# Four GNN layers on one Trainium2 core: graph attention applied ahead of its weight, score terms as row sums, norm shifts on GpSimd, and a new instruction order

## The chip, the core and the metric

The kernel runs on one core of one Trainium2 chip. The metric is device time in microseconds (us) of one execution; of several runs the median is taken. In the profile, PE is TensorE's matmuls, PEld its weight loads, DVE is VectorE, ACT is ScalarE, POOL is GpSimd and SP is SyncE, which here only issues DMAs.

## The reference, cut to what matters

The input x holds 128 graphs of 128 nodes with 256 features, and one 128x128 adjacency matrix `adj` serves all of them. Four layers follow each other; each normalizes its input, applies a ReLU, and adds its result to the input. The third, graph attention, is the one whose arithmetic the change reorders.

```
def layer_L2(h, W, a, beta, mask):
    hw = h @ W
    s1, s2 = hw @ a[:F], hw @ a[F:]
    e = leaky_relu(s1[:, :, None] + s2[:, None, :], 0.2) * mask
    att = softmax(e, axis=2)
    return elu(att @ hw + beta * hw)

h = relu(layernorm(x)); x = x + L0(h, ...)   # 8-head masked attention, projection, layernorm
h = relu(layernorm(x)); x = x + L1(h, ...)   # (adj.T * q k^T), rows divided by their norm, times v
h = relu(layernorm(x)); x = x + L2(h, ...)   # graph attention, above
h = relu(layernorm(x)); x = x + L3(h, ...)   # (adj @ h) @ weight + bias
```

## The kernel before, in words

Two graphs form a pair, and 64 pairs go through the four layers as a software pipeline. One pair's work is cut into steps, and in one turn of the main loop each engine does one step of each of about ten different pairs: in turn t, the name `p3` is pair t-3, and `on[3]` says whether it exists. The order of all instructions on each engine is written out by hand in the function `step` of that engine. Semaphores link the engines. An engine executes strictly in that order, so a wait holds up all that is written behind it. DVE's `step` of turn t+1 runs beside PE's of turn t for most of the work: the pair that DVE calls p1 is then PE's p0.

PSUM has 8 banks, four of them in the tile `mid`, whose four banks take the attention scores of the four row groups. All other products share these banks, and `bank_free` waits for the last reader of a bank.

The steps that matter here, for one pair:

- `moments` (DVE: two `bn_stats`, two `bn_aggr`) and `inverse_root` (POOL: `var_eps`, then `rstd` by a power) make a norm's mean and scale. A small DVE instruction makes `shift` = -mean * rstd (lines 792, 849, 814, 858 for norms 0, 1, 2, 3). ACT then writes the normalized rows z (two instructions per pair), PE transposes them (`transposes`, 4), ACT writes the high part `h_t_hi` with the ReLU, and DVE or POOL the low part `h_t_lo`.
- `product` is a product in two parts (high and low) with 3 matmuls for each of two 128-row pieces. `rows` and `columns` take 12 such matmuls of 256 columns per pair.
- Scores (line 365, 32 small matmuls) go to `mid`; `least_masked` on DVE (line 751, four groups r of four instructions) adds the mask and takes the minimum; ACT's `exps` (line 562) make `probs` and their sums; POOL divides by the sums; PE transposes (line 356); ACT copies to `probs_t`; PE multiplies with the values (line 377, `heads_times_values`).
- Graph attention: z2 is transposed (4 PE transposes), `h_t[2]` is made in two parts, `rows` gives hw with two further columns for the terms s1 and s2 (12 matmuls of 258 columns), ACT copies hw (line 681, two instructions), PE spreads the s2 term (line 431), ACT applies the leaky ReLU, POOL the mask, DVE and ACT the softmax, PE transposes it (line 496), and att times hw is one fp32 product (line 523, 4 records of 256 columns).
- Last layer: adj times h3 (line 450, 8 records), `y_t` in two parts, `rows` with w_out (`y_bank`), and the sum `x4` (line 872).

## Time and profile before

| quantity | value |
|---|---|
| median of 3 runs | 1450.76 us (1449.37 to 1451.83) |
| the profiled execution's own time | 1449.63 us |
| its span, first to last instruction | 1447.8 us |
| granted TensorE clock, mean | 0.993 |
| PE, PEld busy | 1393.4 us, 1321.1 us |
| DVE, ACT, POOL busy | 1235.4 us, 1297.7 us, 973.2 us |
| instructions | 45196 |

Read busy time on PE with care: a matmul record overlaps the next one, so starts of successive records say more than their lengths. The profile's views used below are the busy table, the chain of work that ended last, the busy time by stretch (windows), the timeline of one engine, the waits, and the groups of instructions by line with shapes kept apart.

### The profile page before, as it was taken

What the parts mean: (1) busy time and instruction counts of PE and PEld (TensorE: products, weight loads), DVE (VectorE), ACT (ScalarE), POOL (GpSimd) and SP (SyncE); (2) the same over time, 40 slices, a digit from 0 to 9 for tenths busy, and PEclk for the clock granted to TensorE, in tenths of its full rate; (3) what the DMA queues carried; (4) which work ended last, traced back from release to release, by engine and by line L of the source; (5) the groups of instructions that cost most, each with busy time, mean ns of one, the idle gap of its engine ahead of it and who ended that gap; (6) DMA issues with size and microseconds to landing.
All of it is one profiled execution on the core that took longest, in us unless ns stands there. A gap on an engine that the chain in (4) does not pass through costs nothing.

```text
span 1447.8 us, 45196 instructions
## 1 busy us (share of the span) xinstructions
PE 1393.4 (96%) x14088; PEld 1321.1 (91%) x14088; DVE 1235.4 (85%) x5648; ACT 1297.7 (90%) x4166; POOL 973.2 (67%) x1299
## 2 busy tenths in 40 slices
PE   5899999999999999999999999999999999999996
PEld 4799999999999999999999999999999999999985
DVE  3788889889889888888888888898898898898885
ACT  4899999999999999999999999999999999999973
POOL 4567667667667667667667667667667667667652
PEclk9999999999999999999999999999999999999998
DMA  3000000100001000101000001000101000101000
GB/s 113 17 17 16 24 21 26 31 20 28 31 19 29 31 18 31 31 17 31 31 17 31 31 17 31 31 17 31 31 17 31 31 17 31 31 16 38 16 23 31
DMA packets 38109, 39.74 MB, mean 27 GB/s; under 512 B 2416, under 2 KB 37488, under 8 KB 37872
## 3 DMA queue, kind: packets, MB, share of 16 engines
q1 hardware_dynamic: 37872, 36.84, 8.4%
q8 instruction: 117, 1.92, 0.6%
q14 instruction: 120, 0.98, 0.2%
HBM read 20.05 MB, written 16.78 MB: 25 GB/s over the span
## 4 chain that ended last, share of the span: by engine, by line
POOL 40%; DVE 30%; issue 20%; PE 7%; ACT 2%; SPq 1%; DVEq 0%; POOLq 0%; DMA 0%; ACTq 0%
DVE masked L751 10%; POOL rstd L952 7%; POOL h_t_lo L972 7%; DVE stats L741 6%; POOL probs L979 4%; POOL probs L1010 4%; POOL probs L960 4%; POOL probs L976 4%; POOL inv_norm L965 3%; POOL xb L1008 3%; PE mid L321 3%; DVE shift L814 3%; DVE y_t_lo L806 2%; POOL rel_sq L1004 2%; DVE neg_max L751 2%
## 5 line engine op out<-in xcount | busy, mean ns | idle before, releaser
L562 ACT ACTIVATE probs<-masked,neg_max 128x128 f32<-128x128 f32 x1024 | 396.7, 396 | 0.0
L952 POOL TENSOR_TENSOR rstd<-var_eps,minus_half 128x2 f32<-128x2 f32 x320 | 245.2, 766 | 25.1
L751 DVE CUSTOM_DVE_ANT_0 masked<-mid,mask 128x128 f32<-128x128 f32 x1024 | 234.0, 283 | 2.3 <-issue 2.2
L1004 POOL TENSOR_TENSOR rel_sq<-rel 128x256 f32<-128x256 f32 x64 | 39.3, 613 | 264.2 <-DVE rel L844 264.2
L562 ACT ACTIVATION_READ_ACCUMULATOR probs<-masked,neg_max 128x1 f32 x1024 | 200.1, 195 | 0.0
L356 PE MATMUL bank<-ident,probs 128*128 128x128 f32 x1024 | 143.4, 273 | 0.5 <-POOL probs L979 0.5
L741 DVE BATCH_NORM_STATS2 stats<-x 128x6 f32<-128x256 f32 x384 | 138.8, 403 | 3.8 <-DMA x<-in_x 3.5
L766 DVE SCALAR_TENSOR_TENSOR h_t_lo<-bank,h_t_hi 128x512 fp32r<-128x512 f32 x64 | 44.3, 691 | 105.3 <-ACT h_t_hi L644 105.3
L356 PEld LDWEIGHTS bank<-ident,probs 128*128 128x128 f32 x1024 | 115.9, 141 | 1.3 <-POOL probs L979 0.8
L644 ACT ACTIVATE h_t_hi<-bank 128x512 fp32r<-128x512 f32 x64 | 38.2, 597 | 80.0 <-PE mid L321 78.7
L972 POOL TENSOR_TENSOR h_t_lo<-h_t_full,h_t_hi 128x512 fp32r<-128x512 f32 x64 | 108.1, 1689 | 0.8 <-ACT h_t_full L660 0.8
L965 POOL TENSOR_TENSOR inv_norm<-sum_sq,minus_half 128x2 f32<-128x2 f32 x64 | 45.3, 708 | 78.6 <-DVE sum_sq L881 78.5
L950 POOL TENSOR_TENSOR var_eps<-mean_var,eps 128x2 f32<-128x2 f32 x320 | 69.4, 217 | 41.5 <-DVE mean_var L745 41.3
L1008 POOL TENSOR_TENSOR xb<-x,b_proj_beta 128x512 f32<-128x512 f32 x64 | 82.7, 1293 | 20.4 <-DVE o_res L854 13.4
L321 PE MATMUL bank<-h_t_hi,w_qkv_hi 128*128 128x256 f32 x256 | 84.8, 331 | 5.7 <-DVE h_t_lo L766 5.7
L745 DVE BATCH_NORM_AGGREGATE mean_var<-stats 128x2 f32<-128x6 f32 x640 | 77.6, 163 | 13.8
L615 ACT ACTIVATE z<-x,shift,rstd 128x256 f32<-128x256 f32 x128 | 69.9, 594 | 21.0 <-DVE shift L814 20.8
L321 PE MATMUL mid<-w_proj_hi,o_t_hi 128*128 128x256 f32 x256 | 78.9, 308 | 8.5 <-DVE o_t_lo L822 3.6
L450 PEld LDWEIGHTS bank<-adj_t_sb,h 128*128 128x128 f32 x512 | 63.2, 194 | 24.3 <-issue 20.7
L1000 POOL TENSOR_TENSOR x3b<-x_up,b_out_less 128x512 f32<-128x512 f32 x64 | 82.4, 1287 | 3.2 <-DVE x L872 3.2
L450 PE MATMUL bank<-adj_t_sb,h 128*128 128x128 f32 x512 | 73.3, 287 | 11.5 <-ACT probs_t L578 8.7
L751 DVE DVE_READ_ACCUMULATOR2_ANT neg_max<- 128x1 f32 x1024 | 82.2, 80 | 0.0
(160 smaller groups left out, 5991.2 us busy)
## 6 DMA issues: line engine op xcount, KB each, us to landing
x<-in_x SPq DMA_DIRECT2D x64, 256.0 KB, 3.0
out_x<-x SPq DMA_DIRECT2D x64, 256.0 KB, 3.2
w_qkv_sb<-in_w_qkv SPq DMA_DIRECT2D x1, 768.0 KB, 5.0
w_v_sb<-in_w_v_t SPq DMA_DIRECT2D x1, 256.0 KB, 5.3
w_proj_sb<-in_w_proj SPq DMA_DIRECT2D x1, 256.0 KB, 5.5
w_q_sb<-in_w_q SPq DMA_DIRECT2D x1, 256.0 KB, 6.1
w_k_sb<-in_w_k SPq DMA_DIRECT2D x1, 256.0 KB, 6.5
w_gat_x<-in_w_gat SPq DMA_DIRECT2D x1, 256.0 KB, 6.1
```

Source lines behind the costliest of these rows:

```text
L321: last = pe.matmul(dst, pick_l(lhs_t[a], c), pick_r(rhs[b], c), start=n == 0, stop=n == len(terms) - 1)
L356: last = pe.transpose(dst[:, s * N:(s + 1) * N], probs[:, r, s], ident[:])
L450: last = pe.matmul(y_t_bank[:, (c * 2 + b) * N:(c * 2 + b + 1) * N], h3[:, b, c * 128:(c + 1) * 128], adj_t_sb[:], start=True, stop=True)
L562: last = act.activation(probs[:, r, s], masked[:, r, s], ACT.Exp, scale=-1.0, bias=neg_max[:, r, s:s + 1], accum_out=sums[:, r, s:s + 1])
L741: dve.bn_stats(stats[:, k, b], src[:, b]).then_inc(ln_stats[k], 1)
L745: dve.bn_aggr(mean_var[:, k, b], stats[:, k, b]).then_inc(ln_moments[k], 1)
L751: last = dve.tensor_tensor_reduce(out=masked[:, r, s], in0=mid[:, r, s * N:(s + 1) * N], in1=mask[:], scale=1.0, scalar=LARGE, op0=ALU.add ...
L952: pool.tensor_tensor(rstd[:, k], var_eps[:, k], minus_half[:], ALU.pow).then_inc(ln_rstd[k], 1)
L965: pool.tensor_tensor(inv_norm[:], sum_sq[:], minus_half[:], ALU.pow).then_inc(inv_norm_ready, 1)
L972: pool.tensor_tensor(flat(h_t[1][1]), flat(h_t1_full), flat(h_t[1][0]).bitcast(f32), ALU.subtract)\
L1000: pool.tensor_tensor(x3b[:], x3_up[:, i8], both(b_out_less), ALU.add).then_inc(x3b_ready, 1)
L1008: pool.tensor_tensor(xb[:], x0[:, i1], both(b_proj_beta), ALU.add).then_inc(xb_ready, 1)
```

## The change

What it does, part by part:

1. **Graph attention.** ACT writes h2 = relu(norm(x2)) row by row (`h2`, two turns of it are held) instead of z2; the transposes of z2, `h_t[2]` and the product hw go away. PE forms m = h2 under att, already transposed (8 records of 128 columns); m is split in a high part (ACT) and a low part (DVE), and `rows` with w_gat (12 matmuls of 256 columns) gives att h2 W + beta h2 W.
2. **Score terms.** s1 and s2 are row sums of h2 times w_gat a1 and w_gat a2. Four DVE instructions per pair multiply and sum 256 elements each (`s12`). The rows of w_gat a (`wa_rows`) are made once, in turn 4, by four PE transposes and an ACT copy.
3. **Shifts.** POOL makes `neg_mean` and `shift` for norms 0 to 3 (two small instructions more per norm); DVE's four shift instructions go away.
4. **Orders and banks.** `STREAMS` is 9 instead of 10, nearly every bank is given anew, and all four `step` functions are written in another order. PE's and SP's loops had 73 turns with nothing in PE's last one; they have 72. The product of `fold` moves from turn 2 to turn 1.

```diff
-    STREAMS = 10
+    STREAMS = 9
...
-            def step(t, par, on):
...
+                if on[6]:
+                    pe.wait_ge(att_t_ready, done(p6))
+                    pe.wait_ge(h2_ready, done(p6))
+                    bank_free(pe, (probs_t_ready[3], p2, 1), (v1_ready, p4, 1))
+                    for c in range(C):
+                        for b in range(2):
+                            last = pe.matmul(m_bank[:, (c * 2 + b) * N:(c * 2 + b + 1) * N], h2[:, i6, b, c * 128:(c + 1) * 128],
+                                             att_t[:, b], start=True, stop=True)
+                    last.then_inc(m_psum, 1)
+                if on[3]:
+                    pe.wait_ge(z_ready[1], done(p3))
+                    bank_free(pe, (max_ready[0], p1, 1), (probs_t_ready[0], p2, 1), (g_ready, p4, 1),
+                              (e_leaky_ready, p6, 2))
+                    transposes(z1_bank, z[1]).then_inc(h_t_psum[1], 1)
...
-                    rows([hw0_bank[:, 0:DX], hw1_bank[:, 0:DX]], h_t[2], w_gat_p, 0, DX).then_inc(hw_psum, 1)
...
+                if on[6]:
+                    pe.wait_ge(m_lo_ready, done(p6))
+                    bank_free(pe, (max_ready[2], p1, 1))
+                    rows(halves(u_bank), m_t_p, w_gat_p, 0, D).then_inc(u_psum, 1)
...
+                if on[5]:
+                    dve.wait_ge(h2_ready, done(p5))
+                    wait_before(dve, e_leaky_ready, p5, 2)
+                    dve.memset(s12_turn[:], 0.0)
+                    for b in range(2):
+                        for j in range(2):
+                            last = dve.tensor_tensor_reduce(out=s12_prod[:, b, j], in0=h2[:, i5, b], in1=wa_rows[:, j], scale=1.0, scalar=0.0,
+                                                            op0=ALU.mult, op1=ALU.add, accum_out=s12[:, b, j:j + 1])
+                    last.then_inc(s12_ready, 1)
+                if on[6]:
+                    dve.wait_ge(m_hi_ready, done(p6))
+                    dve.tensor_tensor(flat(m_t_p[1]), m_bank, flat(m_t_p[0]).bitcast(f32), ALU.subtract).then_inc(m_lo_ready, 1)
...
+            def inverse_root_and_shift(k, p, shift_k):
+                pool.wait_ge(ln_moments[k], done(p, 2))
+                pool.tensor_tensor(var_eps[:, k], mean_var[:, k, :, 1], eps[:], ALU.add).then_inc(ln_eps[k], 1)
+                pool.tensor_tensor(neg_mean[:, k], mean_var[:, k, :, 0], minus_one[:], ALU.mult).then_inc(ln_neg_mean[k], 1)
+                pool.wait_ge(ln_eps[k], done(p))
+                pool.tensor_tensor(rstd[:, k], var_eps[:, k], minus_half[:], ALU.pow).then_inc(ln_rstd[k], 1)
+                pool.wait_ge(ln_neg_mean[k], done(p))
+                pool.wait_ge(ln_rstd[k], done(p))
+                return pool.tensor_tensor(shift_k[:], neg_mean[:, k], rstd[:, k], ALU.mult)
```

TensorE, before, around the scores of a turn in the middle of the run (probs: transposes of the attention's probabilities; adj_t_sb: the adjacency product of the last layer; k_t,q_t: scores; probs_t,v: heads times values; w_v: values of the second layer):

```order
L321 MATMUL bank<-h_t_hi,w_qk_lo 128x256
L356 MATMUL bank<-ident,probs 128x128 x8
L450 MATMUL bank<-adj_t_sb,h 128x128 x4
L365 MATMUL mid<-k_t,q_t 128x128 x16
L377 MATMUL bank<-probs_t,v 32x128 x16
L321 MATMUL bank<-w_v_hi,h_t_hi 128x256
```

TensorE, now, around the scores (g_t,h_t_full: the relation product of the second layer; att_t,h: the new product m; ident,z behind it: the transposes of z1):

```order
L330 MATMUL mid<-h_t_hi,w_qkv_lo 128x256
L524 MATMUL mid<-adj_t_sb,h 128x128 x4
L365 MATMUL mid<-ident,probs 128x128 x4
L538 MATMUL bank<-g_t,h_t_full 128x128 x4
L365 MATMUL bank<-ident,probs 128x128 x8
L552 MATMUL bank<-ident,att_norm 128x128 x2
L374 MATMUL mid<-k_t,q_t 128x128 x16
L386 MATMUL bank<-probs_t,v 32x128 x16
L445 MATMUL bank<-att_t,h 128x128 x4
L346 MATMUL mid<-ident,z 128x128 x4
```

The adjacency product no longer stands between the last transposes of probabilities and the scores but ahead of three other products, and behind the heads come m and then a transposition into a bank of `mid` that the scores have just filled.

GpSimd, before, from the last norm of a turn on:

```order
L950 TENSOR_TENSOR var_eps<-mean_var,eps 128x2
L952 TENSOR_TENSOR rstd<-var_eps,minus_half 128x2
L1000 TENSOR_TENSOR x3b<-x_up,b_out_less 128x512
L1004 TENSOR_TENSOR rel_sq<-rel 128x256
L1008 TENSOR_TENSOR xb<-x,b_proj_beta 128x512
L1010 TENSOR_TENSOR probs<-probs,inv_sums 128x512
```

GpSimd, now, from the squares of the relation product on:

```order
L992 TENSOR_TENSOR rel_sq<-rel 128x256
L964 TENSOR_TENSOR var_eps<-mean_var,eps 128x2
L965 TENSOR_TENSOR neg_mean<-mean_var,minus_one 128x2
L967 TENSOR_TENSOR rstd<-var_eps,minus_half 128x2
L970 TENSOR_TENSOR shift<-neg_mean,rstd 128x2
L999 TENSOR_TENSOR x3b<-x_up,b_out_less 128x512
L1003 TENSOR_TENSOR h_t_lo<-h_t_full,h_t_hi 128x512
L1008 TENSOR_TENSOR inv_norm<-sum_sq,minus_half 128x2
L1012 TENSOR_TENSOR xb<-x,b_proj_beta 128x512
```

Each of the four norms has two more instructions, and the low part h_t_lo now follows x3b.

VectorE, now, from x_up (the third layer's sum) to the first group of minima of the next scores (ISA: the instructions of `least_masked`):

```order
L850 SCALAR_TENSOR_TENSOR x_up<-mid,x_exp 128x512
L854 TENSOR_TENSOR y_t_lo<-mid,y_t_hi 128x512
L759 BN_STATS stats<-x 128x6 x2
L761 MEMSET turn 1x1
L763 BN_AGGR mean_var<-stats 128x2 x2
L862 TENSOR_TENSOR rel<-bank,adj_sb 128x256
L759 BN_STATS stats<-x_up 128x6 x2
L761 MEMSET turn 1x1
L763 BN_AGGR mean_var<-stats 128x2 x2
L767 MEMSET mask_turn 1x1
L769 ISA masked,neg_max<-mid,mask 128x128
```

Before, y_t_lo stood directly ahead of the first group of minima (of row group 3); now two norms' moments and rel stand between the two, and the first group is row group 0.

## Rows read from the trace of the kernel before

**Rows 1.** The page, part 1: busy us, share of the span, instructions.
```profile
PE 1393.4 (96%) x14088; PEld 1321.1 (91%) x14088; DVE 1235.4 (85%) x5648; ACT 1297.7 (90%) x4166; POOL 973.2 (67%) x1299
```
**Rows 2.** The page, part 4: chain that ended last, shares of the span.
```profile
POOL 40%; DVE 30%; issue 20%; PE 7%; ACT 2%; SPq 1%; DVEq 0%; POOLq 0%; DMA 0%; ACTq 0%
```
**Rows 3.** Windows: PE, PEld, DVE, ACT, POOL busy; clock, DMA share, GB/s.
```profile
300.00:522.50 222.50, 220.06 (x2240) 209.40 (x2240) 194.77 (x889) 204.93 (x663) 155.07 (x204) 1.00 0.09 28
```
**Rows 4.** Timeline of PE, one turn: start, us, line, operands, count.
```profile
812.60 1.03 PE L356 MATMUL bank<-ident,probs 128*128 128x128 f32 x8
813.79 1.13 PE L450 MATMUL bank<-adj_t_sb,h 128*128 128x128 f32 x8 [0.16 <-ACT probs_t L578]
814.85 1.17 PE L365 MATMUL mid<-k_t,q_t 32*128 32x128 f32 x32
815.95 1.08 PE L377 MATMUL bank<-probs_t,v 128*32 128x128 f32 x32
816.96 0.39 PE L321 MATMUL bank<-w_v_hi,h_t_hi 128*128 128x256 f32 x1
...
822.57 0.38 PE L496 MATMUL bank<-ident,att_norm 128*128 128x128 f32 x2
822.79 0.60 PE L337 MATMUL bank<-ident,z 128*128 128x128 f32 x4
823.23 0.60 PE L337 MATMUL mid<-ident,z 128*128 128x128 f32 x4
...
825.92 1.03 PE L523 MATMUL mid<-hw,att_t 128*128 128x256 f32 x4
826.79 1.02 PE L530 MATMUL bank<-v,rel 128*128 128x256 f32 x4
```
**Rows 5.** Waits, 700 to 1100 us: who waited for whom, total us, times, longest.
```profile
PEld bank L450 <- issue: 6.9, 19, 0.4
...
PEld mid L321 <- DVE o_t_lo L822: 5.1, 18, 0.4
```
**Rows 6.** Timeline of DVE, then one row each of POOL's and ACT's.
```profile
813.46 0.74 DVE L741 BATCH_NORM_STATS2 stats<-x_up 128x6 f32<-128x256 f32 x2
...
814.40 0.39 DVE L800 TENSOR_REDUCE e_neg_max<-e_mask 128x2 f32<-128x256 f32 x1
...
815.65 0.66 DVE L806 TENSOR_TENSOR y_t_lo<-bank,y_t_hi 128x512 fp32r<-128x512 f32 x1
816.24 0.28 DVE L751 CUSTOM_DVE_ANT_0 masked<-mid,mask 128x128 f32<-128x128 f32 x1
...
817.08 1.02 DVE L814 SCALAR_TENSOR_TENSOR shift<-mean_var,rstd 128x2 f32<-128x2 f32 x1
...
816.80 1.28 POOL L1000 TENSOR_TENSOR x3b<-x_up,b_out_less 128x512 f32<-128x512 f32 x1
...
814.95 0.64 ACT L593 ACTIVATE y_t_hi<-bank 128x512 fp32r<-128x512 f32 x1
```
**Rows 7.** Groups by line and shape, 700 to 1100 us; the last from the first turns.
```profile
L681 ACT ACTIVATE hw<-bank 128x258 f32<-128x258 f32 x19 | 7.7, 408 | 0.0
L792 DVE SCALAR_TENSOR_TENSOR shift<-mean_var,rstd 128x2 f32<-128x2 f32 x19 | 12.9, 678 | 3.5 <-POOL rstd L952 3.5
L858 DVE SCALAR_TENSOR_TENSOR shift<-mean_var,rstd 128x2 f32<-128x2 f32 x18 | 2.7, 152 | 0.0
L950 POOL TENSOR_TENSOR var_eps<-mean_var,eps 128x2 f32<-128x2 f32 x94 | 20.1, 214 | 9.1 <-DVE mean_var L745 9.1
...
18.39 0.41 DVE L728 CUSTOM_DVE_ANT_0 wa_prod<-w_gat_x,a_gat_bc 128x256 f32<-128x256 f32 x1
```
**Rows 8.** Timeline of PE: the scores of pairs 0, 8, and 62.
```profile
18.83 1.17 PE L365 MATMUL mid<-k_t,q_t 32*128 32x128 f32 x32 [0.78 <-ACT k_t L574]
...
161.82 1.17 PE L365 MATMUL mid<-k_t,q_t 32*128 32x128 f32 x32
...
1337.29 1.17 PE L365 MATMUL mid<-k_t,q_t 32*128 32x128 f32 x32
```

More of the change, by code:

```diff
@@ L102, in gnn_stack @@
         z = [sb(f"z{k}", [128, 2, D]) for k in range(3)]
-        h_t = [parts(f"h_t{k}", [128, C, 2 * N]) for k in range(3)]
+        h_t = [parts(f"h_t{k}", [128, C, 2 * N]) for k in range(2)]
         h_t1_full = sb("h_t1_full", [128, C, 2 * N])
@@ L445, in step @@
-                if on[8]:
-                    pe.wait_ge(h3_ready, done(p8))
-                    bank_free(pe, (probs_t_ready[2], p2, 1), (x2_ready, p5, 2), (att_t_ready, p7, 1))
+                    bank_free(pe, (att_t_ready, p6, 1))
+                    rows(halves(v_bank), h_t[0], w_qkv_p, 2 * D, D).then_inc(v0_psum, 1)
+                if on[4]:
+                    pe.wait_ge(rel_sq_ready, done(p4))
+                    for b in range(2):
+                        last = pe.matmul(rel_bank[:, 256 + b:257 + b], rel_sq[:, b], ones[:, 0:1], start=True, stop=True)
+                    last.then_inc(sum_sq_psum, 1)
@@ new lines, in step @@
+                if on[8]:
+                    pe.wait_ge(y_lo_ready, done(p8))
+                    bank_free(pe, (max_ready[1], p1, 1), (y_lo_ready, p8, 1), (x2_ready, p5, 2))
+                    rows(halves(y_bank), y_t_p, w_out_p, 0, D).then_inc(y_psum, 1)
+                if on[2]:
+                    pe.wait_ge(o_lo_ready, done(p2))
+                    bank_free(pe, (o_lo_ready, p2, 1), (probs_t_ready[2], p2, 1), (probs_t_ready[1], p2, 1))
+                    for b in range(2):
+                        last = product(o_bank[:, b * D:(b + 1) * D], o_t_p, w_proj_p,
+                                       lambda a, c: a[:, b, c], lambda a, c: a[:, c])
+                    last.then_inc(o_psum, 1)
@@ new lines, in step @@
+                if on[4]:
+                    pe.wait_ge(v1_ready, done(p4))
+                    pe.wait_ge(rel_ready, done(p4))
+                    bank_free(pe, (x4_ready, p8, 1), (max_ready[1], p1, 1), (y_lo_ready, p8, 1))
+                    for b in range(2):
+                        last = pe.matmul(rel_v_bank[:, b * D:(b + 1) * D], rel[:, b], v1[:, b], start=True, stop=True)
+                    last.then_inc(rel_v_psum, 1)
+                if on[3]:
+                    pe.wait_ge(h_lo_ready[1], done(p3))
+                    bank_free(pe, (e_leaky_ready, p5, 2), (h1_full_ready, p3, 1), (max_ready[0], p1, 1),
+                              (probs_t_ready[0], p2, 1))
+                    columns(g_bank, w_qk_p, 0, h_t[1]).then_inc(g_psum, 1)
@@ L510, in step @@
-                if on[4]:
-                    pe.wait_ge(rel_sq_ready, done(p4))
-                    for b in range(2):
-                        last = pe.matmul(rel_bank[:, 256 + b:257 + b], rel_sq[:, b], ones[:, 0:1], start=True, stop=True)
-                    last.then_inc(sum_sq_psum, 1)
-                if on[3]:
-                    pe.wait_ge(z_ready[1], done(p3))
-                    bank_free(pe, (o_ready, p2, 1), (max_ready[3], p1, 1), (k_ready, p1, 1))
-                    transposes(z1_bank, z[1]).then_inc(h_t_psum[1], 1)
@@ new lines, in step @@
+                if on[5]:
+                    act.wait_ge(att_t_psum, done(p5))
+                    wait_before(act, m_psum, p5)
+                    act.activation(att_t[:].rearrange("p b n -> p (b n)"), att_bank[:, 0:2 * N], ACT.Copy).then_inc(att_t_ready, 1)
+                if on[2]:
+                    act.wait_ge(shift_ready[1], done(p2))
+                    wait_before(act, h_t_psum[1], p2)
+                    for b in range(2):
+                        last = act.activation(z[1][:, b], x1[:, i2, b], ACT.Identity, bias=shift[1][:, b:b + 1],
+                                              scale=rstd[:, 1, b:b + 1])
+                    last.then_inc(z_ready[1], 1)
@@ new lines, in step @@
+                if on[4]:
+                    act.wait_ge(shift_ready[2], done(p4))
+                    wait_two_before(act, m_psum, p4)
+                    for b in range(2):
+                        last = act.activation(h2[:, i4, b], x2[:, i4, b], ACT.Relu, bias=shift[2][:, b:b + 1], scale=rstd[:, 2, b:b + 1])
+                    last.then_inc(h2_ready, 1)
+                if on[1]:
+                    act.wait_ge(heads_psum, done(p1))
+                    wait_before(act, o_psum, p1)
+                    act.activation(o_t_p[0][:].rearrange("p b c n -> p (b c n)"), heads_bank, ACT.Copy).then_inc(o_hi_ready, 1)
@@ L875, in step @@
+                i0, i1, i2, i3, i4, i5, i6, i7, i8 = [(par + s) % 2 for s in range(STREAMS)]
                 if on[3]:
```

705 lines of the change are left out of this document (320 added, 385 removed).

## The prediction, made before the changed kernel had run

> **What bounds the kernel now.** I read the busy table first [rows 1]: PE 96%, PEld 91%, ACT 90%, DVE 85%, POOL 67%. A matmul's record overlaps the next one's, so the 96% may flatter; but the weight loads alone fill 209.40 of 222.50 us in the middle of the run [rows 3], at full clock. Next the chain that ended last [rows 2]: it runs over POOL (40%) and DVE (30%) and hardly over PE (7%), which says that the hand-written order links all engines in a ring and does not say that POOL is short of time: POOL is busy 155.07 of 222.50 us there [rows 3]. Then the turn. The scores of pairs 8 and 62 start at 161.82 and 1337.29 us [rows 8], 54 turns apart, so a turn is 21.77 us. ACT leaves (222.50 - 204.93) / 222.50 x 21.77 = 1.7 us of it free, DVE 2.7 us, POOL 6.6 us [rows 3].
>
> On PE I look for real gaps. A group of four transposes takes 0.44 us from start to start (822.79 to 823.23) [rows 4]; the eight transposes at 812.60 should take 0.88 us, yet the next record starts after 1.19 us: 0.31 us of waiting, and PEld shows the same place as 6.9 us in 19 turns, 0.36 each [rows 5]. The projection's wait for o_t_lo is 5.1 us in 18 turns, 0.28 each [rows 5]. The first gives 0.31 us, the second I take at 0.24 because the record behind it is not delayed by the whole gap. So PE idles about 0.55 us a turn, at most 0.36 + 0.28 = 0.64, and its work is 21.2 us of 21.77. **PE's issue is the bound**, and a change can gain in only two ways: less PE work, or fewer of these gaps.
>
> **The change, part by part.** All prices are for one pair, which is one turn.
>
> PE loses the four transposes of z2, 0.44 us, and the fp32 product att hw, 0.87 us (825.92 to 826.79) [rows 4]. It gains m, 8 records of 128 columns like the adjacency product: 1.06 us (813.79 to 814.85) [rows 4]. Twelve matmuls of 258 columns become twelve of 256: nothing. Sum: -0.44 - 0.87 + 1.06 = **-0.25 us**.
>
> ACT loses two copies of hw, 2 x 0.41 us [rows 7], and one 512-wide copy, and gains one of the same width for m: about -0.8 us by their lengths, less where they overlap. Two instructions for z2 become two for h2. ACT then has some 2.3 us free.
>
> DVE loses four shifts, of 0.68, 1.02 and twice 0.15 us [rows 6, 7], 2.0 us. It gains four sums over 256 products. Such an instruction with two SBUF operands took 0.41 us in the first turns [rows 7]: 1.64 us. One low part goes and one comes. So about -0.3 us, and still 2.5 to 3 us free.
>
> POOL gains eight small instructions, priced by var_eps at 0.21 us [rows 7]: 1.7 us, or 2.2 us with a wait on the result before each shift. It keeps over 4 us.
>
> No engine but PE is near the turn's length; what remains is whether the new order makes PE wait. I laid PE's new turn end to end with the prices above, the scores 1.10 and heads 1.01 us [rows 4], and looked at the four tightest hand-overs. For a result to show on the next engine I put an estimated 0.2 us, since a group's records outlast the next group's start by 0.16 us (0.60 - 0.44) [rows 4].
>
> First, the copies of the last transposed probabilities to the heads. Between them PE has the two transposes of att_norm (0.22) and the scores (1.10), 1.32 us [rows 4]. The last copy needs about 0.2 us for the result to show, a 0.64 us copy [rows 6], and perhaps 0.2 us behind the copy before it: 1.04. Slack 0.3 us.
>
> Second, z1's transposes go to the bank of `mid` that the scores filled, so `least_masked(0)` must be done. PE has the heads and m in between, 1.01 + 1.06 = 2.07 us; DVE needs 0.25 + 0.84 (816.24 to 817.08 [rows 6]) = 1.1 us. Slack 0.9 us, if DVE is there when the scores end.
>
> Third, whether it is. From the adjacency product's end to the scores' end PE has 0.44 + 1.06 + 0.88 + 0.22 + 1.10 = 3.70 us. ACT and DVE have the copy y_t_hi 0.64 plus 0.2, y_t_lo 0.59, moments 0.94 (813.46 to 814.40), rel about 0.35 (half a 512-wide instruction) and moments 0.94 [rows 6]: 3.66 us. DVE arrives as the scores end. This is the tight stretch, and the 0.9 us of slack covers it.
>
> Fourth, m's two parts to the product with w_gat. Between m and that product PE has z1, v, the sums of squares, y, the projection, z0 and the s2 spread, over 5.8 us; the copy and low part need about 1.5 us, and DVE's four sums 1.64 us. No wait.
>
> So I expect both old gaps to go and small new ones of 0.15 us in sum: 21.77 - 0.25 - 0.55 + 0.15 = **21.1 us**. Bounds: 20.85 us without any gap, 21.5 us with gaps as large as now.
>
> Head and tail. The scores of pair 8 stand at 161.82 us now [rows 8], and they are in the first full turn of either order. The first turn still ends with scores near 19 us, since it needs the same load, norm and two products. POOL's late constants move into turn 1, ahead of the norm of pair 1, but the probabilities of pair 0 no longer wait behind them, so I put the fill at 162 +- 8 us. From the scores of pair 63 (161.82 + 55 x 21.77 = 1359 us) to the end are 88.7 us now. The name STREAMS suggests a shorter drain, but PE's work ended in turn 71 before and does so now, and a pair's way from z0's transposes to y is 7.9 turns both times. I keep 88.7 us.
>
> Span: 162 + 55 x 21.1 + 88.7 = 1411.2 us. The profiled execution's time was 1449.63 - 1447.8 = 1.8 us above its span, and the median 1.1 us above that: **1414 us**.
>
> GpSimd and VectorE hinder each other here: a DVE shift of 0.15 us took 1.02 us beside POOL's x3b, and both ended together (818.10 and 818.08) [rows 6, 7]. The Trainium skill, GPSIMD Engine Reference, section Key points, says that GpSimd shares its SBUF interfaces with VectorE and contends with VectorE instructions in a 2-port mode or with two SBUF inputs. The trace agrees for the small shifts. By that rule the removal of the shifts helps and the four new sums, which read two SBUF operands each, hurt; with each of the four held as long as the 1.02 us shift, DVE would lose 4 x (1.02 - 0.41) = 2.4 us, nearly all that it has free, which makes the second rival below likelier.
>
> **The rivals.**
>
> *The gaps stay.* PE does less, but new hand-overs cost what the old ones did: 21.5 us, 162 + 1182.5 + 88.7 + 2.9 = 1436 us. For it: the first hand-over has 0.3 us of slack only. Against it: I find no second one under 0.8 us.
>
> *DVE comes late to the minima, slower.* DVE is held beside POOL by the new sums or the moments, arrives at `least_masked(0)` late, and PE stands before z1's transposes with everything behind them. The first 0.9 us are covered. PE may lose 0.55 + 0.25 = 0.8 us a turn before the kernel is slower, so this decides from 1.7 us of lateness on; at 2.0 us a turn is 20.97 + 1.1 = 22.1 us, and the time 162 + 1215.5 + 88.7 + 2.9 = 1469 us. For it: up to 2.4 us of holding, as above, and two moments that moved ahead of the minima. Against it: the four sums stand behind the minima, with over 2 us free until the next place that PE waits for, and the moments and y_t_lo read one SBUF operand or PSUM.
>
> *It does not do what it says.* The ring, not PE, sets the turn, and its length in the new order happens to be the old one: 21.75 us, 1450 us. Against it: the four hand-overs above are what the ring consists of.
>
> **How the numbers follow.** Forecast 0.56 (turn 20.9 to 21.3 us: 1398 to 1426 us with the head's 8 us partly used), the gaps stay 0.24, slower 0.14, same turn 0.06. The range reaches from 1396 us (20.85 us a turn, a shorter fill) to 1441 us (the gaps stay, a little longer head) and leaves out 0.20. Faster by over 0.2% (about what a measurement here can tell from no change): 0.80; within: 0.06; slower: 0.14.
>
> **What would show it.** Right: the scores start 21.0 to 21.3 us apart; PEld's waits in the middle sum to under 0.4 us a turn; m takes about 1.06 us and the product u follows without a wait; DVE waits for the scores, not PE for neg_max. Wrong: PE before z1's transposes waits for DVE neg_max (second rival), PE before the heads waits for ACT probs_t (first); a sum of products (now 0.41 us) that takes 0.8 us or more; scores of pair 8 later than 170 us, or a drain longer than 97 us.

## The result, and the profile after

The changed kernel takes 1485.3 us, median of 4 runs (1484.4 to 1488.67), against 1450.58 us before (1449.37 to 1451.83, 4 runs): a ratio of 1.025 with a 95% interval of 1.0233 to 1.0266. It is slower by 35 us. I had forecast 1414 us and given "slower" 0.14. The profiled execution has a span of 1483.3 us at a mean granted clock of 0.992, so the clock is not the reason.

First the busy table of the changed kernel (page, part 1: busy us, share of the span, instructions), which answers [rows 1].

```profile
PE 1377.0 (93%) x14092; PEld 1301.5 (88%) x14092; DVE 1401.8 (95%) x5966; ACT 1283.1 (86%) x4039; POOL 1056.7 (71%) x1812
```

DVE was the least busy engine but POOL at 85%, and is now the busiest at 95%; PE fell from 96% to 93%. Then the chain of work that ended last (page, part 4, shares of the span by engine, then by line), against [rows 2].

```profile
DVE 72%; issue 17%; PE 6%; ACT 3%; POOL 1%; DMA 0%; DVEq 0%; SPq 0%; ACTq 0%; POOLq 0%
```

Before, the chain ran over POOL 40% and DVE 30%. Now it lies mostly on DVE. The window in the middle of the run (columns as in [rows 3]) is about ten turns long:

```profile
300.00:525.40 225.40, 214.73 (x2223) 203.82 (x2224) 222.20 (x948) 201.67 (x634) 165.76 (x286) 1.00 0.08 25
```

DVE is busy 222.20 of 225.40 us at full clock: DVE is the bound. The scores of three pairs (PE timeline: start, us, line, operands, count, idle before and who ended it) give the turn, as [rows 8] did. They are pairs 0, 8 and 63.

```profile
19.09 1.17 PE L374 MATMUL mid<-k_t,q_t 32*128 32x128 f32 x32 [0.78 <-ACT q_t L680]
...
163.78 1.17 PE L374 MATMUL mid<-k_t,q_t 32*128 32x128 f32 x32 [1.06 <-DVE y_t_lo L854]
...
1390.44 0.82 PE L374 MATMUL mid<-k_t,q_t 32*128 32x128 f32 x18 [0.66 <-DVE y_t_lo L854]
```

The turn is (1390.44 - 163.78) / 55 = 22.30 us where it was 21.77. Fill: 163.78 us, 2 us later than before. Tail: 1483.3 - 1390.44 = 92.9 us, 4 more. The 55 turns bring 29.5 of the 35.5 us by which the span grew. What matters is why a turn takes 22.3 us instead of 21.1.

The groups of DVE by line and shape, 300 to 1300 us (busy us, mean ns of one, idle before), name the instructions that grew. After:

```profile
L884 DVE CUSTOM_DVE_ANT_0 s_prod<-h,wa_rows 128x256 f32<-128x256 f32 x180 | 147.5, 871 | 0.0
...
L832 DVE SCALAR_TENSOR_TENSOR x<-o_gam,rstd,o_res 128x256 f32<-128x256 f32 x90 | 77.1, 894 | 1.1
...
L807 DVE SCALAR_TENSOR_TENSOR x_exp<-u_exp,x 128x512 f32<-128x512 f32 x45 | 53.0, 1177 | 0.0
```

Before, the two of these that existed (L787 is the first layer's sum, now L832; L892 the third layer's x_exp, now L807):

```profile
L787 DVE SCALAR_TENSOR_TENSOR x<-o_gam,rstd,o_res 128x256 f32<-128x256 f32 x92 | 40.2, 478 | 0.0
...
L892 DVE SCALAR_TENSOR_TENSOR x_exp<-u_exp,x 128x512 f32<-128x512 f32 x46 | 31.8, 692 | 18.4 <-ACT u_exp L664 18.4
```

The four sums of the score terms take 0.87 us each and not the 0.41 that I had priced; the first layer's sum went from 0.478 to 0.894, twice a turn, and x_exp from 0.692 to 1.177 us, though of these two only the place in the order changed. Per turn that is 4 x 0.46 + 2 x 0.416 + 0.485 = 3.2 us of DVE time that is in no line of the diff. All three lines read two operands from SBUF.

Over 1000 us in the middle, before and then after (columns as in [rows 3]; the third busy time is DVE's), the windows show it as well:

```profile
300.00:1300.00 1000.00, 988.70 (x10111) 940.40 (x10111) 880.05 (x4040) 925.10 (x2985) 695.10 (x920) 1.00 0.09 26
```

```profile
300.00:1300.00 1000.00, 952.46 (x9835) 903.80 (x9836) 985.94 (x4170) 895.49 (x2830) 734.35 (x1255) 1.00 0.09 26
```

The timelines of one turn show what they wait for. DVE of the changed kernel, from o_t_lo to m_t_lo:

```profile
814.80 0.69 DVE L876 TENSOR_TENSOR o_t_lo<-bank,o_t_hi 128x512 fp32r<-128x512 f32 x1
815.41 1.37 DVE L884 CUSTOM_DVE_ANT_0 s_prod<-h,wa_rows 128x256 f32<-128x256 f32 x1
...
816.71 0.41 DVE L884 CUSTOM_DVE_ANT_0 s_prod<-h,wa_rows 128x256 f32<-128x256 f32 x1
...
817.05 0.41 DVE L884 CUSTOM_DVE_ANT_0 s_prod<-h,wa_rows 128x256 f32<-128x256 f32 x1
...
817.40 1.50 DVE L884 CUSTOM_DVE_ANT_0 s_prod<-h,wa_rows 128x256 f32<-128x256 f32 x1
...
818.83 0.68 DVE L889 TENSOR_TENSOR m_t_lo<-bank,m_t_hi 128x512 fp32r<-128x512 f32 x1
```

POOL of the same kernel in the same stretch:

```profile
815.20 1.29 POOL L999 TENSOR_TENSOR x3b<-x_up,b_out_less 128x512 f32<-128x512 f32 x1
817.31 1.30 POOL L1003 TENSOR_TENSOR h_t_lo<-h_t_full,h_t_hi 128x512 fp32r<-128x512 f32 x1 [0.82 <-ACT h_t_full L616]
```

The first sum starts beside x3b, which ends at 816.49, and the sum ends at 816.78, some 0.3 us behind it. The next two have POOL idle beside them, but for the last 0.15 us of the third, and take 0.41. The fourth meets h_t_lo, which ends at 818.61, and ends at 818.90, again 0.3 us behind it. It looks as if a held sum starts its work only when POOL's instruction is done. Over the 45 turns from 300 to 1300 us, one of the first two sums is held in every turn and the fourth in 36. The record o_t_lo, which reads PSUM and SBUF, lies beside x3b for its last 0.29 us and takes the usual 0.69 us.

The other two lines meet POOL's work in the same way. DVE, one turn, and below it POOL (L811 and L832 are two instructions in one row):

```profile
801.58 0.66 DVE L784 SCALAR_TENSOR_TENSOR h_t_lo<-bank,h_t_hi 128x512 fp32r<-128x512 f32 x1
...
802.48 1.18 DVE L807 SCALAR_TENSOR_TENSOR x_exp<-u_exp,x 128x512 f32<-128x512 f32 x1
803.58 0.87 DVE L811 SCALAR_TENSOR_TENSOR o_gam<-o,mean_var,gamma_bc 128x256 f32<-128x256 f32 x2
...
805.37 1.71 DVE L832 SCALAR_TENSOR_TENSOR x<-o_gam,rstd,o_res 128x256 f32<-128x256 f32 x2
```

```profile
801.38 0.73 POOL L1016 TENSOR_TENSOR e_mask<-e_leaky,adj_sb 128x256 f32<-128x256 f32 x1
802.08 1.03 POOL L1019 TENSOR_TENSOR probs<-probs,inv_sums 128x512 f32<-128x512 f32 x1
803.08 0.64 POOL L958 TENSOR_TENSOR var_eps<-mean_var,eps 128x2 f32<-128x2 f32 x1
803.79 0.82 POOL L960 TENSOR_TENSOR rstd<-var_eps,minus_half 128x2 f32<-128x2 f32 x1
...
805.59 1.22 POOL L1029 TENSOR_TENSOR probs<-probs,inv_sums 128x512 f32<-128x512 f32 x1
```

x_exp starts while POOL has 0.63 us left of its probabilities, and ends 0.55 us behind them. The first of the two L832 instructions comes ahead of POOL's and the second meets it; POOL's own record is longer too, 1.22 us beside the 1.03 of the other.

Three more readings of these rows matter. DVE's h_t_lo (L784) is the same operation as x_exp and writes as many elements to SBUF, but takes one operand from PSUM: it lies beside POOL's e_mask for 0.53 us and takes its usual 0.66. So neither the operation nor the write is what is held. POOL's var_eps, of two elements, comes second to x_exp: it takes 0.64 us where it takes 0.20 elsewhere, and ends 0.06 us behind x_exp. And not every overlap is a hold: the second o_gam (0.47 us, two operands in SBUF) lies wholly inside the record of POOL's rstd, a power of two elements that takes 0.82 us, and is no longer for it.

Last the waits between 700 and 1100 us (who waited for whom, total us, times, longest), against [rows 5].

```profile
PEld mid L374 <- issue: 22.0, 18, 1.4
PE mid L374 <- DVE y_t_lo L854: 18.3, 18, 1.2
```

PE waits a good microsecond a turn, ahead of the scores, whose bank of `mid` is free only when DVE has made y_t_lo from it. There is no wait of z1's transposes for the minima.

### The profile page after: what moved, and what is told of

Same layout as the page of the kernel before. It is cut to its first block, busy times and chain, and to the rows that moved or that the text cites. A ratio compares the mean times of both kernels' runs of the same rounds, so it can differ in the third digit from the quotient of the medians.

```text
span 1483.3 us, 45972 instructions
## 1 busy us (share of the span) xinstructions
PE 1377.0 (93%) x14092; PEld 1301.5 (88%) x14092; DVE 1401.8 (95%) x5966; ACT 1283.1 (86%) x4039; POOL 1056.7 (71%) x1812
## 4 chain that ended last, share of the span: by engine, by line
DVE 72%; issue 17%; PE 6%; ACT 3%; POOL 1%; DMA 0%; DVEq 0%; SPq 0%; ACTq 0%; POOLq 0%
DVE stats L759 13%; DVE masked L769 7%; DVE s_prod L884 7%; DVE x L832 6%; DVE x_exp L807 4%; DVE mean_var L763 3%; DVE x L819 3%; DVE y_t_lo L854 2%; DVE neg_max L769 2%; DVE x_up L850 2%; DVE o_res L910 2%; DVE o L912 2%; DVE h_t_lo L784 2%; DVE x L906 2%; DVE o_gam L811 2%
## 5 line engine op out<-in xcount | busy, mean ns | idle before, releaser
L884 DVE CUSTOM_DVE_ANT_0 s_prod<-h,wa_rows 128x256 f32<-128x256 f32 x256 | 197.3, 823 | 0.4 <-issue 0.4
L967 POOL TENSOR_TENSOR rstd<-var_eps,minus_half 128x2 f32<-128x2 f32 x256 | 176.6, 690 | 0.0
L374 PE MATMUL mid<-k_t,q_t 32*128 32x128 f32 x2048 | 75.1, 282 | 59.6 <-DVE y_t_lo L854 57.2
L374 PEld LDWEIGHTS mid<-k_t,q_t 32*128 32x128 f32 x2048 | 64.7, 186 | 72.9 <-issue 71.8
L365 PE MATMUL bank<-ident,probs 128*128 128x128 f32 x768 | 105.6, 274 | 7.2 <-POOL probs L1019 6.8
L832 DVE SCALAR_TENSOR_TENSOR x<-o_gam,rstd,o_res 128x256 f32<-128x256 f32 x128 | 108.7, 888 | 1.5
L330 PE MATMUL mid<-h_t_hi,w_qk_hi 128*128 128x256 f32 x256 | 83.5, 326 | 0.0
L330 PE MATMUL mid<-w_out_hi,y_t_hi 128*128 128x256 f32 x256 | 78.9, 308 | 3.2 <-DVE y_t_lo L854 3.2
L1029 POOL TENSOR_TENSOR probs<-probs,inv_sums 128x512 f32<-128x512 f32 x64 | 78.1, 1220 | 3.9 <-DVE inv_sums L824 3.8
L715 ACT ACTIVATE o_t_hi<-bank 128x512 fp32r<-128x512 f32 x64 | 38.2, 596 | 48.5 <-PE bank L386 47.8
```

Source lines behind the costliest of these rows:

```text
L330: last = pe.matmul(dst, pick_l(lhs_t[a], c), pick_r(rhs[b], c), start=n == 0, stop=n == len(terms) - 1)
L365: last = pe.transpose(dst[:, s * N:(s + 1) * N], probs[:, r, s], ident[:])
L374: last = pe.matmul(mid[:, r, s * N:(s + 1) * N], q_t[at, hc, b * N:(b + 1) * N], k_t[at, hc, b * N:(b + 1) * N], start=True, stop=True, ti ...
L832: dve.scalar_tensor_tensor(x1[:, i3, b], o_gam[:, b], rstd[:, LN_O, b:b + 1], o_res[:, b], ALU.mult, ALU.add).then_inc(x1_ready, 1)
L884: last = dve.tensor_tensor_reduce(out=s12_prod[:, b, j], in0=h2[:, i5, b], in1=wa_rows[:, j], scale=1.0, scalar=0.0, op0=ALU.mult, op1=ALU ...
L967: pool.tensor_tensor(rstd[:, k], var_eps[:, k], minus_half[:], ALU.pow).then_inc(ln_rstd[k], 1)
```

## The experiments

The theory from the two traces I call the theory of exclusion: a DVE instruction with two operands in SBUF and a POOL instruction don't run at the same time; whichever comes second waits for the other's end and its record grows by the wait. The rstd of the rows above is an exception, which the experiments leave open; x3b, h_t_lo and the probabilities, POOL's long instructions, are what they turn on. Its rivals were that the new order as such is too long, that the sums are slow in themselves, and that the eight new small POOL instructions a turn are what costs.

**One operand instead of two.** The sums read h2 alone; the score terms lose their weights.

```diff
-                            last = dve.tensor_tensor_reduce(out=s12_prod[:, b, j], in0=h2[:, i5, b], in1=wa_rows[:, j], scale=1.0, scalar=0.0,
-                                                            op0=ALU.mult, op1=ALU.add, accum_out=s12[:, b, j:j + 1])
+                            last = dve.tensor_reduce(s12[:, b, j:j + 1], h2[:, i5, b], op=ALU.add, axis=AX.X)
```

> The changed kernel, with each of DVE's four products-and-sums per pair replaced by a plain sum over the same 256 elements of h2: one SBUF operand instead of two, so the attention's score terms are left unweighted. Theory H (a DVE instruction with two SBUF operands and a GpSimd instruction exclude each other, whoever comes second waits): the four fall from 0.87 us each to about 0.4, DVE wins 1.9 us a turn, PE becomes the bound, turn 22.30 -> 21.2 us, time about 1424 us. Rival O (the hand-written order, not DVE's time, sets the turn through y_t_lo ahead of the scores): the turn stays within 0.2 us of 22.30 and the time within 10 us of 1485.

Measured: 1409.05 us, ratio to before 0.9725 (0.971 to 0.974), and 76 us under the changed kernel. The group of the sums, 300 to 1300 us:

```profile
L884 DVE TENSOR_REDUCE s<-h 128x1 f32<-128x256 f32 x188 | 65.5, 411 | 0.0
```

One turn of its timelines, first DVE (the second row is three sums), then POOL:

```profile
797.48 0.42 DVE L884 TENSOR_REDUCE s<-h 128x1 f32<-128x256 f32 x1
797.81 1.06 DVE L884 TENSOR_REDUCE s<-h 128x1 f32<-128x256 f32 x3
```

```profile
797.26 1.29 POOL L998 TENSOR_TENSOR x3b<-x_up,b_out_less 128x512 f32<-128x512 f32 x1
```

They stand at the same place in the order, run right beside x3b, and take 0.411 us on average, which is what the two-operand form takes when POOL is idle. The turn is 21.0 us. So it is neither the order nor the number of POOL instructions; four instructions of the same length at the same place, without a second SBUF operand, bring the whole loss back. (The plain sum also writes no products to SBUF; h_t_lo and x_exp above show that the write is not what is held.) The gain was larger than I had expected because the turn fell to 21.0 us and not to 21.2; that PE would be the bound again I had expected.

**Without x3b on POOL.** POOL doesn't add the bias of the last layer; x4 adds x3 itself.

```diff
-                if on[8]:
-                    wait_before(pool, x4_ready, p8)
-                    pool.wait_ge(x3_ready, done(p8))
-                    pool.tensor_tensor(x3b[:], x3_up[:, i8], both(b_out_less), ALU.add).then_inc(x3b_ready, 1)
...
-                    dve.wait_ge(x3b_ready, done(p8))
+                    dve.wait_ge(x3_ready, done(p8))
```

> The changed kernel without GpSimd's addition x3b (the last bias, less one, is left out of the result; DVE's x4 reads x3 directly). DVE's program has the same instructions. H: the first of the four sums, held for 0.96 us until x3b ends, takes 0.41 us; the turn falls by about 0.9 us to 21.4, time about 1435 us. Rival S (such a sum is slow in itself, or beside any traffic of ACT and PE): the four sums keep a mean of 0.87 us and the time stays within 10 us of 1485.

Measured: 1406.9 us, ratio 0.9711 (0.9695 to 0.9727). All sums take 0.42 us, the fourth too, although h_t_lo is still there:

```profile
L884 DVE CUSTOM_DVE_ANT_0 s_prod<-h,wa_rows 128x256 f32<-128x256 f32 x188 | 68.6, 420 | 0.0
```

I had expected the second hold to stay. With the first one gone the sums are over at 797.87 us in one turn, and h_t_lo starts at 798.27, so it was the first hold that pushed the fourth sum into the second. The first layer's sum and x_exp are as slow as in the changed kernel (0.880 and 1.174 us), and the kernel is fast all the same: their 1.3 us a turn are paid out of time that DVE has to spare once the sums are short.

**Shifts back on DVE.** Part 3 of the change is undone; parts 1, 2 and 4 stay. Four small shifts return to DVE, and POOL loses the eight small instructions. One of the four places:

```diff
-                    inverse_root_and_shift(0, p0, shift[0]).then_inc(shift_ready[0], 1)
+                    inverse_root(0, p0)
...
+                if on[0]:
+                    dve.wait_ge(ln_rstd[0], done(p0))
+                    wait_before(dve, z_ready[0], p0)
+                    dve.scalar_tensor_tensor(shift[0][:], mean_var[:, 0, :, 0], -1.0, rstd[:, 0], ALU.mult, ALU.mult)\
+                       .then_inc(shift_ready[0], 1)
```

> The changed kernel with part 3 undone: the four shifts are DVE instructions again, GpSimd has eight small instructions less. H: DVE, the bound, gets four instructions of 0.15 us that can be held up to 1 us each: the turn grows by 0.6 to 2 us, time 1518 to 1590 us, most likely 1530. Rival P (the eight new GpSimd instructions cost the change its gain): the time falls below 1475 us.

Measured: 1460.28 us, ratio 1.0081 (1.0066 to 1.0096). I had expected it far above the changed kernel and it is 25 us below. The timelines say why. DVE, one turn:

```profile
799.24 1.01 DVE L887 SCALAR_TENSOR_TENSOR shift<-mean_var,rstd 128x2 f32<-128x2 f32 x1
...
800.85 0.41 DVE L904 CUSTOM_DVE_ANT_0 s_prod<-h,wa_rows 128x256 f32<-128x256 f32 x1
```

and POOL's two long instructions near it:

```profile
798.94 1.29 POOL L1019 TENSOR_TENSOR x3b<-x_up,b_out_less 128x512 f32<-128x512 f32 x1
802.42 1.30 POOL L1023 TENSOR_TENSOR h_t_lo<-h_t_full,h_t_hi 128x512 fp32r<-128x512 f32 x1 [2.19 <-ACT h_t_full L616]
```

Without its eight small instructions POOL reaches x3b earlier, and x3b now meets one small shift (0.99 us on average instead of 0.15) and none of the sums, which take 0.414 us. The theory of exclusion stands, but my price of this experiment assumed that POOL's work would stay where it was. DVE now carries 0.99 + 3 x 0.15 = 1.4 us of shifts, is busy 985.60 of 1000 us, and the turn is 21.64 us, (1336.25 - 167.44) / 54. What part 3 did in the changed kernel is thereby plain: it took the shifts off DVE and pushed x3b, and the fourth sum behind it, into holds of 1.8 us. A short record runs some 0.08 us into the next one, so counted from start to start the four shifts cost DVE 0.91 + 0.08 + 0.08 + 0.07 = 1.1 us. The difference to the 1.8 us, 0.7 us, is the 0.66 us between the two turns.

**Part 3 alone on the kernel before.** Its DVE has no sums with two operands.

```diff
-                    inverse_root(1, p3)
+                    inverse_root_and_shift(1, p3, shift[1]).then_inc(shift_ready[1], 1)
...
-                    dve.scalar_tensor_tensor(shift[0][:], mean_var[:, 0, :, 0], -1.0, rstd[:, 0], ALU.mult, ALU.mult)\
-                       .then_inc(shift_ready[0], 1)
```

> The kernel before with part 3 alone: the shifts on GpSimd, DVE without them, nothing else moved. H: DVE loses 2.0 us a turn (1.02 + 0.68 + 2 x 0.15), PE's gaps of 0.55 us close at least in part: turn 21.2 to 21.7 us, time 1415 to 1448, most likely 1435 us. Rival P (the longer chain over GpSimd delays the norms): slower than 1453 us.

Measured: 1427.94 us, ratio 0.9856 (0.9841 to 0.987), a turn of (1338.45 - 160.72) / 55 = 21.41 us. The expectation held. The busy times of this kernel, 300 to 1300 us:

```profile
300.00:1300.00 1000.00, 994.75 (x10286) 954.39 (x10286) 824.72 (x3930) 935.72 (x3037) 757.25 (x1312) 1.00 0.09 27
```

PE is busy 994.75 of 1000 us and DVE only 824.72. In the order of the kernel before, eight more small instructions on POOL cost nothing, which with the run of one operand, where they all stay, ends that rival; part 3 alone makes the kernel before 21 us faster.

**The sums behind x4.** Everything is computed. On DVE the sums stand where POOL waits for o_res; PE's spread of s2, the leaky ReLU, the mask and its maximum follow later, and the minima of row group 2 move ahead of the copy of the sums of squares.

```diff
+                if on[5]:
+                    dve.wait_ge(h2_ready, done(p5))
+                    wait_before(dve, e_leaky_ready, p5, 2)
...
+                    last.then_inc(s12_ready, 1)
                 if on[2]:
                     dve.wait_ge(xb_ready, done(p2))
```

> The changed kernel with DVE's four sums moved behind x4, into the stretch in which GpSimd waits for o_res; PE's spread of s2 behind the product u, ACT's leaky ReLU, GpSimd's mask and DVE's maximum of it later in the same way. Nothing is left out. H: the sums fall to 0.45 us or less on average, turn 21.0 to 21.4 us, time 1405 to 1430 us. Rival O (the order is tight, a move of this chain makes ACT and PE wait): the sums are short and the time is above 1450 us all the same.

Measured: 1436.53 us, ratio 0.9921 (0.9905 to 0.9938), outside what I had expected (1405 to 1430 us) and under the rival's 1450 us. The sums are free, but others are held in their place. Groups of DVE, 300 to 1300 us:

```profile
L832 DVE SCALAR_TENSOR_TENSOR x<-o_gam,rstd,o_res 128x256 f32<-128x256 f32 x94 | 88.3, 977 | 0.2 <-issue 0.2
L905 DVE CUSTOM_DVE_ANT_0 s_prod<-h,wa_rows 128x256 f32<-128x256 f32 x188 | 68.6, 420 | 0.0
L807 DVE SCALAR_TENSOR_TENSOR o_gam<-o,mean_var,gamma_bc 128x256 f32<-128x256 f32 x94 | 63.5, 714 | 0.0
...
L803 DVE SCALAR_TENSOR_TENSOR x_exp<-u_exp,x 128x512 f32<-128x512 f32 x47 | 38.8, 826 | 0.0
```

o_gam, 0.473 us until now, takes 0.714, the first layer's sum 0.977, x_exp 0.826. Moving DVE's instructions shifts all that follow against POOL's list, and the holds move with them. The turn is 21.29 us. The way from the sums to the softmax is longer too, and the two causes were not separated.

**x3b behind h_t_lo.** Everything is computed; one POOL instruction moves.

```diff
-                if on[8]:
-                    wait_before(pool, x4_ready, p8)
-                    pool.wait_ge(x3_ready, done(p8))
-                    pool.tensor_tensor(x3b[:], x3_up[:, i8], both(b_out_less), ALU.add).then_inc(x3b_ready, 1)
                 if on[3]:
                     pool.wait_ge(h1_full_ready, done(p3))
...
+                if on[8]:
+                    wait_before(pool, x4_ready, p8)
+                    pool.wait_ge(x3_ready, done(p8))
+                    pool.tensor_tensor(x3b[:], x3_up[:, i8], both(b_out_less), ALU.add).then_inc(x3b_ready, 1)
```

> The changed kernel with one GpSimd instruction moved: x3b stands behind h_t_lo instead of ahead of it, nothing is left out. H: GpSimd waits for ACT's h_t_full while DVE makes its four sums, so none of them is held, they take 0.41 to 0.45 us each, the turn falls from 22.30 to about 21.1 us, as in the run without x3b, and the time is 1405 to 1418 us, most likely 1410. Rival W (the run without x3b won because GpSimd had 1.3 us less work a turn): the time is above 1460 us.

Measured: 1426.71 us, ratio 0.9848 (0.9833 to 0.9864); the sums take 0.42 us as expected, but the time is 9 us above the range. One row of DVE's timeline shows what took the place:

```profile
811.96 0.69 DVE L906 TENSOR_TENSOR x<-mid,x3b 128x512 f32<-128x512 f32 x1 [0.66 <-issue]
```

x4 needs x3b, which POOL now ends at 811.87, and DVE stands idle for 0.66 us a turn. A hold had become a wait. The turn is 21.27 us.

**x3b in POOL's gap.** In the changed kernel POOL waits 1.1 us between the norm of h2 and that of z0 (norm 0; the expectation below calls it z1), beside y_t_lo, moments and rel on DVE, none of which reads two operands from SBUF. x3's data have been there since the turn before.

```diff
+                if on[8]:
+                    wait_before(pool, x4_ready, p8)
+                    pool.wait_ge(x3_ready, done(p8))
+                    pool.tensor_tensor(x3b[:], x3_up[:, i8], both(b_out_less), ALU.add).then_inc(x3b_ready, 1)
                 if on[0]:
                     wait_before(pool, z_ready[0], p0)
                     inverse_root_and_shift(0, p0, shift[0]).then_inc(shift_ready[0], 1)
...
-                if on[8]:
-                    wait_before(pool, x4_ready, p8)
-                    pool.wait_ge(x3_ready, done(p8))
-                    pool.tensor_tensor(x3b[:], x3_up[:, i8], both(b_out_less), ALU.add).then_inc(x3b_ready, 1)
```

> The changed kernel with one instruction of GpSimd moved: x3b (x3 plus the bias, 1.29 us) stands between the norm of h2 and the norm of z1, where the changed kernel's GpSimd waits 1.1 us for the moments and VectorE runs instructions with one operand in SBUF. Everything is computed. Theory of exclusion (a VectorE instruction with two operands in SBUF and a GpSimd instruction don't run at once, the second waits): no sum of the score terms overlaps it, so the four take 0.42 us each (0.87 on average in the changed kernel), and x4 doesn't wait for x3b, as it did by 0.66 us a turn with x3b behind h_t_lo. The turn falls from 22.3 to the 21.0 at which TensorE is the bound: 1403 to 1412 us, most likely 1408. The instructions of VectorE that take x1 (0.88) and x_exp (1.17) stay held. Rival: x3b now sits ahead of the norm of z1 and delays its shift, z1_t and the pair's first projections by up to 0.3 us, and the time stays at 1420 to 1430 as with x3b behind h_t_lo.

Measured: 1410.41 us, median of 5 (1408.93 to 1411.96), ratio to before 0.972 (0.9707 to 0.9734). It computes all that the changed kernel computes, with the same instructions, one of them at another place, is 75 us faster than it and 40 us faster than the kernel before. Busy times and the groups of DVE, 300 to 1300 us:

```profile
300.00:1300.00 1000.00, 987.30 (x10446) 957.13 (x10448) 966.50 (x4406) 944.77 (x3000) 777.00 (x1333) 1.00 0.09 27
```

```profile
L832 DVE SCALAR_TENSOR_TENSOR x<-o_gam,rstd,o_res 128x256 f32<-128x256 f32 x96 | 80.5, 880 | 0.3 <-issue 0.3
L884 DVE CUSTOM_DVE_ANT_0 s_prod<-h,wa_rows 128x256 f32<-128x256 f32 x188 | 68.6, 420 | 0.0
...
L807 DVE SCALAR_TENSOR_TENSOR x_exp<-u_exp,x 128x512 f32<-128x512 f32 x48 | 56.4, 1175 | 0.0
```

The sums are free, no wait has replaced the hold, and the other two lines are as slow as in the changed kernel. The turn is (1320.77 - 165.28) / 55 = 21.01 us. So taking the holds off the sums, 4 x (0.871 - 0.420) = 1.8 us of DVE time a turn, is enough to bring the whole loss back; 1.3 us of it show in the turn, the rest DVE now spends idle (3.35% of 21.01 is 0.7 us, against 0.3 us idle in the changed kernel).

**x3b in two halves.** To see what a held instruction waits for, x3b is cut in two at the place where the changed kernel has it. Everything is computed.

```diff
-                    pool.tensor_tensor(x3b[:], x3_up[:, i8], both(b_out_less), ALU.add).then_inc(x3b_ready, 1)
+                    pool.tensor_tensor(x3b[:, 0], x3_up[:, i8, 0], b_out_less[:], ALU.add)
+                    pool.tensor_tensor(x3b[:, 1], x3_up[:, i8, 1], b_out_less[:], ALU.add).then_inc(x3b_ready, 1)
```

> The changed kernel with GpSimd's x3b cut in two instructions of 128x256 (by the row of rel_sq and e_mask some 0.61 to 0.74 us each) at the same place. Everything is computed. If the exclusion is one between single instructions, VectorE gets its turn when the first half ends: no sum lasts over 1.1 us where the first was held to 1.37, though a second sum may be held by the second half, and the time moves little, 1470 to 1488, most likely 1480. If VectorE is held until GpSimd's queue is empty or idle, or if what counts is the GpSimd work in sum, the held sum stays at 1.3 to 1.5 us and the time at 1485 to 1492. If the number of GpSimd instructions is what costs, it is slower than the changed kernel by some 0.1 us a turn, 1490.

Measured: 1478.25 us, ratio 1.0192 (1.0178 to 1.0206), in the middle of what exclusion between single instructions gave. The timeline of DVE in the turn where the lists meet most closely (2 of 46 turns look like this; the common form stands below):

```profile
834.64 0.42 DVE L884 CUSTOM_DVE_ANT_0 s_prod<-h,wa_rows 128x256 f32<-128x256 f32 x1
...
834.99 0.97 DVE L884 CUSTOM_DVE_ANT_0 s_prod<-h,wa_rows 128x256 f32<-128x256 f32 x1
...
835.89 0.95 DVE L884 CUSTOM_DVE_ANT_0 s_prod<-h,wa_rows 128x256 f32<-128x256 f32 x1
...
836.77 1.50 DVE L884 CUSTOM_DVE_ANT_0 s_prod<-h,wa_rows 128x256 f32<-128x256 f32 x1
```

and of POOL beside it:

```profile
834.68 0.99 POOL L999 TENSOR_TENSOR x3b<-x_up,b_out_less 128x256 f32<-128x256 f32 x1 [0.20 <-issue]
835.62 0.93 POOL L1000 TENSOR_TENSOR x3b<-x_up,b_out_less 128x256 f32<-128x256 f32 x1
836.54 1.45 POOL L1004 TENSOR_TENSOR h_t_lo<-h_t_full,h_t_hi 128x512 fp32r<-128x512 f32 x1
```

The two lists take turns, instruction by instruction. The first sum was there first and runs its 0.42 us; the first half waits for it and takes 0.99 us, where in 44 of 46 turns it finds the way free and takes 0.74. The second sum waits for the first half, the second half for the second sum, the third sum for the second half, h_t_lo (1.29 us undisturbed) for the third sum, the fourth sum for h_t_lo. In the common turn (43 of 46) the first half comes first, the first sum is held behind it (0.81 us), the second half behind that sum (0.91), the second sum behind the second half (0.94), and the third sum takes 0.41 with POOL idle. None of the sums beside a half takes over 1 us. So an instruction waits for the one on the other side to end, not for an idle queue, and the price of a hold is set by the length of that one instruction.

## Why the prediction was wrong, step by step

**Which step failed.** It was the price of DVE: "It gains four sums over 256 products. Such an instruction with two SBUF operands took 0.41 us in the first turns: 1.64 us. ... So about -0.3 us, and still 2.5 to 3 us free." The row I took it from [rows 7] comes from the kernel's first turns, where no long POOL instruction lay beside it. In the steady turn the four take 3.48 us. The other part of what DVE's account missed lies in two lines that the prediction didn't speak of: the first layer's sum (+0.83 us a turn) and x_exp (+0.49 us), which the new order put beside POOL's probabilities. The runs show that without the sums' part the loss is gone although these two stay; whether it would also be gone without these two and with the sums held was not run. Expected were -0.3 us on DVE. The rows of after give 3.48 us of sums - 2.01 us of shifts + 0.83 + 0.49 = +2.8 us, and the windows agree: DVE was busy 85% of 21.77 us in the page and 880.05 of 1000 us in the middle, 19.2 us a turn, and is busy 985.94 of 1000, 22.0 us a turn. Of the 2.7 us that DVE had free, 0.3 are left.

**I had the warning and weighed it too low.** The prediction showed the one small shift that x3b had stretched from 0.15 to 1.02 us [rows 6], and worked out 4 x (1.02 - 0.41) = 2.4 us. Measured were 1.8 us for the sums. The rule that it named stands in the Trainium skill, GPSIMD Engine Reference, section Key points: GpSimd and VectorE share SBUF interfaces and contend when VectorE has two SBUF inputs. The trace agrees: a sum of 0.41 us takes 1.37 beside x3b. What I then did wrong was to price that case as a share of a rival at 0.14 instead of laying POOL's new list beside DVE's. The part of the change section on GpSimd already had what was needed: the sequence norm, x3b, h_t_lo in a row, and x3b of 1.3 us with DVE's sums somewhere near. I laid out PE's turn end to end, but POOL's never.

**The rival that came.** "DVE comes late" was the right mechanism and nearly the right size: a turn of 22.1 us and 1469 us against 22.30 and 1485. The size is partly luck, since it came from 2.0 us of lateness less 0.9 us of slack at a wait that never arose, and left out the 1.3 us of the other two lines. Its place was wrong. Nothing waits for the minima at z1's transposes; PE waits 1.0 us a turn at the scores, for y_t_lo (18.3 us in 18 turns), which is the third hand-over, the one that I had called the tight stretch and then covered by the 0.9 us of slack behind the scores. That slack could not cover it: y_t's bank is one of the four that the scores fill, so y_t_lo has to be done before the scores start and not before they end. And the argument against the rival, that the sums stand behind the minima with 2 us free until PE next needs DVE, was of the wrong kind: once DVE is busy through the whole turn, it doesn't matter where in the turn it loses time.

**What held.** The ends did: the fill was put at 162 +- 8 us and is 163.78, the tail at 88.7 and is 92.9 in the changed kernel and 1410.2 - 1320.77 = 89.4 us where DVE isn't the bound. The turn of 21.1 us was nearly right where the sums are free and nothing else was put in their place: 21.0 in three experiments (21.3 in the two others with free sums, behind x4 and with x3b behind h_t_lo), and the forecast of 1414 us lies 4 us from the 1410.4 of the same instructions with x3b moved. The forecast of the four hand-overs held there but for the third: the waits of that kernel between 700 and 1100 us show 8.8 / 19 = 0.46 us a turn at the scores.

```profile
PEld mid L374 <- issue: 8.8, 19, 0.6
```

So PE's own work is at most about 20.6 us, less than the 20.97 that I had reckoned, and the small gaps are larger than the 0.15 us; the two errors cancelled, and where exactly PE saved the other 0.4 us I did not trace.

**A range too narrow on one side.** 1396 to 1441 us left out a resource whose use could double for a reason that the trace of before showed. With 1.8 to 2.4 us of possible holding on an engine with 2.7 us free, and no look at whether it happens, the range should have reached into the 1470s.

**What stays open.** What limits the 21.01 us of the best version: PE 98.7%, DVE 96.7%, weight loads 95.7% and ACT 94.5% busy lie too close together to name one, and I did not free the first layer's sum and x_exp there. Why the sums behind x4 came out at 1436 us is explained only in part, by the holds that moved.

## What to carry to other kernels

Lay the list of GpSimd and the list of VectorE side by side over a whole turn before you price any VectorE instruction with two operands in SBUF; take its duration from a stretch in which GpSimd runs, or price it as its own length plus what may be left of GpSimd's. Work that one moves to GpSimd to relieve VectorE also moves everything behind it there, and here the 1.3 us instruction that came to lie on four sums took back the whole gain and 35 us more; moving that single instruction into an idle stretch of GpSimd, beside VectorE work that reads PSUM or one operand, gave 75 us. An engine that is 85% busy becomes the bound by a stretch of 0.45 us in four of its instructions and as much in three others.
